# A four-layer graph network on 100,000 nodes: the row numbers of a chunk are copied one round ahead, in two of its stages

## The reference

```python
def _ngcf_conv(x, W1, W2, src, dst, n):          # layer 1, called twice
    norm = rsqrt(deg_out[src] * deg_in[dst])
    msg = (x[src] @ W1 + x[src] * x[dst] @ W2) * norm[:, None]
    return x @ W1 + segment_sum(msg, dst, n)
...
x = layernorm(x + conv(relu(conv(x, W1_1, W2_1)), W1_2, W2_2))
...
# layer 3, the last: attention over edges in both directions and a loop at each node
logits = leaky_relu(s_node[src] + d_node[dst] + e_all, 0.2)
z = exp(logits - segment_max(logits, dst)[dst])
out = segment_sum((z / segment_sum(z, dst)[dst])[:, None] * (x @ W)[src], dst)
x = layernorm(x + out)
```

## Time and profile before

| | |
|---|---|
| median of 3 runs | 10054.14 us (10051.63 to 10055.38) |
| the profiled execution's own time | 10059.48 us |
| its span, first to last instruction | 10057.3 us |
| PE, PEld | 3022.2 us (30%), 2811.3 us (28%) |
| DVE | 6330.4 us (63%) |
| ACT | 2917.7 us (29%) |
| POOL | 6560.1 us (65%) |
| `convolve_edges1`, gathers | from 3055.3 us to 4162 us |
| `finish_edges`, gathers | from 8306.7 us to 9466 us |

### The profile page before, as it was taken

One profiled execution on the slowest core, in us unless ns is written; L12 is line 12 of the kernel. 1 busy time (PEld: TensorE's weight loads), 2 busy tenths in 40 slices (PEclk: granted clock), 3 DMA queues, 4 the chain that ended last, 5 costly groups with the idle time before them and its releaser, 6 DMA issues. The chain is left out here.

```text
span 10057.3 us, 92986 instructions
## 1 busy us (share of the span) xinstructions
PE 3022.2 (30%) x15231; PEld 2811.3 (28%) x15231; DVE 6330.4 (63%) x18443; ACT 2917.7 (29%) x8172; POOL 6560.1 (65%) x6186
## 2 busy tenths in 40 slices
PE   3233002111114666500666634444400002333300
PEld 2132001111114555400655534444400002333300
DVE  8999887666664767500665579999644435666600
ACT  5366234333333444300433312222200002223200
POOL 2334017777776777577777757777677777666577
PEclk7566555555556878755555555555555555665555
DMA  1010271111113544411544511111111113434311
GB/s 53 14 30 24 98 234 26 25 25 25 25 22 101 158 148 155 134 43 50 182 170 169 177 43 48 47 47 47 39 44 45 44 42 105 112 108 115 91 45 40
DMA packets 455154, 791.99 MB, mean 79 GB/s; under 512 B 119922, under 2 KB 149611, under 8 KB 454559
## 3 DMA queue, kind: packets, MB, share of 16 engines
q1 hardware_dynamic: 252126, 560.13, 16.7%
q0 software_dynamic: 188448, 201.53, 9.2%
q10 hardware_dynamic: 14112, 26.10, 0.7%
HBM read 388.06 MB, written 425.04 MB: 81 GB/s over the span
## 5 line engine op out<-in xcount | busy, mean ns | idle before, releaser
L1056 POOL DMA_INDIRECT e_other<-X,e_from_rows x392 | 610.9, 1558 | 279.5 <-DVE e_fin L1343 143.2
L1720 POOL DMA_INDIRECT e_mine<-T,e_from_rows x392 | 400.7, 1022 | 569.3 <-DVE e_from_rows L1767 450.8
L743 POOL COPY sort_spare<-sort_words 128x768 f32<-128x768 f32 x272 | 369.2, 1379 | 606.9 <-DVE sort_words L802 396.9
L3395 POOL DMA_INDIRECT e4s_mine<-XA,e4s_from_rows x392 | 407.9, 1041 | 231.9 <-DVE e4s_from_rows L3449 124.3
L2209 PE MATMUL e_turned<-ident,e_own_x 128*128 128x128 f32 x196 | 54.6, 434 | 1573.6 <-ACT e_own_x L2121 1573.6
L2357 POOL DMA_INDIRECT e_mine<-X,e_from_rows x392 | 406.6, 1037 | 183.1 <-issue 112.5
L3416 POOL DMA_INDIRECT out_rows<-e4s_out,e4s_to_rows x392 | 385.2, 983 | 191.0 <-issue 191.0
L2378 POOL DMA_INDIRECT G<-e_g_slot,e_to_rows x392 | 385.2, 983 | 180.6 <-issue 119.0
L2865 POOL DMA_INDIRECT X<-e_row,e_to_rows x392 | 424.8, 1084 | 119.5 <-issue 116.1
L1070 POOL DMA_INDIRECT X<-e_row,e_to_rows x392 | 401.8, 1025 | 140.9 <-issue 118.2
L3398 POOL DMA_INDIRECT e4s_other<-X,e4s_from_rows x392 | 402.2, 1026 | 129.4 <-issue 127.6
(11 more groups left out here) (693 smaller groups left out, 15698.4 us busy)
## 6 DMA issues: line engine op xcount, KB each, us to landing
XA<-e_n_xa SPq DMA_DIRECT2D x49, 1056.0 KB
e4s_n_xa<-XA SPq DMA_DIRECT2D x49, 1056.0 KB, 6.3
X<-e_n_row SPq DMA_DIRECT2D x49, 576.0 KB
T<-pl_row SPq DMA_DIRECT2D x98, 272.0 KB
X<-e_n_row SPq DMA_DIRECT2D x49, 528.0 KB, 3.0
X<-pl_x ACTq DMA_DIRECT2D x98, 260.0 KB, 2.7
e_n_x<-X SPq DMA_DIRECT2D x49, 520.0 KB
G<-e_n_g SPq DMA_DIRECT2D x49, 512.0 KB, 2.8
```

Source lines behind the costliest of these rows:

```text
L1056: gp.indirect_dma_start(out=other[:, h, j, :], out_offset=None, in_=others[:, :], in_offset=bass.IndirectOffsetOnAxis(ap=from_rows[:, h, 1 ...
L1720: gp.indirect_dma_start(out=mine[:, h, j, :], out_offset=None, in_=g.T0[:, :], in_offset=bass.IndirectOffsetOnAxis(ap=from_rows[:, h, 0, j ...
L3395: gp.indirect_dma_start(out=mine[:, h, j, :], out_offset=None, in_=g.XA[:, :], in_offset=bass.IndirectOffsetOnAxis(ap=from_rows[:, h, 0, j ...
```

## The change

In both stages VectorE's pipeline is called with one more chunk in the round. The new first one, `ahead`, is chunk r of round r, and gets the copy of row numbers; all other parts get the chunks that they got, one round later (`c0` is now chunk r-1, `c1` is r-2, and so on). The copy keeps its place among the parts of the round, and its wait. The other engines' pipelines, the tiles and the semaphores are the same. VectorE's written-out first rounds become one more.

```diff
-                def body(*c):
+                def body(ahead, *c):
                     c0, c1, c2, c3, c4 = c
                     if c3:
                         node_spread(c3)
-                    if c0:
-                        n, h, k = c0.n, c0.slot, c0.k
+                    if ahead:
+                        n, h, k = ahead.n, ahead.slot, ahead.k
                         v.wait_ge(gathered[h], k * 32 * J)
                         v.tensor_copy(from_rows[:, h, :, :], g.index[s][:, 0:2, bass.ds(n * J, J)]).then_inc(from_ready[h], 1)
...
-                stages(v, NCH, RING, SKEW, body)
+                stages(v, NCH, RING, SKEW + 1, body)
...
-                def body(*c):
+                def body(ahead, *c):
                     if c[5]:
                         norm(c[5], J)
...
-                    if c[0]:
-                        n, h, k = c[0].n, c[0].slot, c[0].k
+                    if ahead:
+                        n, h, k = ahead.n, ahead.slot, ahead.k
                         v.wait_ge(gathered[h], k * 32 * J)
                         v.tensor_copy(from_rows[:, h, :, :], g.index[s][:, 0:2, bass.ds(n * J, J)]).then_inc(from_ready[h], 1)
...
-                stages(v, NCH, RING, SKEW, body)
+                stages(v, NCH, RING, SKEW + 1, body)
```

## The result

The changed kernel takes 9892.84 us (median of 4 runs, 9891.55 to 9893.38), the one before 10052.88 us beside it (4 runs, 10042.53 to 10055.38). The ratio is 0.9843, 95% interval 0.9825 to 0.986: faster by 160 us. The forecast was 9916 us, 138 us faster, in a range of 9880 to 9968; the sign and the range hold, and the gain is 22 us larger than the sum said.

The account below looks back on a forecast made before the run. POOL's gathers, waiting for VectorE's copy in both stages, were taken as the bound; 153 - 12 - 3 = 138 us off the profiled 10059.5 gives 9921.5, and 5.3 us less for the median gives 9916 us, range 9880 to 9968.

Parts of the forecast that it names:

- the sum: Both stages: 153 us of waits less 12 for longer gathers and 3 for lag, 138 us faster.
- The bound: Both stages: POOL's gather stream, including its waits for VectorE's copy of row numbers, is in the critical stretch.
- The waits removed, 52 + 101 us: POOL's waits for the copy go, except each stage's first: 52 us in convolve_edges1, 101 us in finish_edges.
- issue price: On POOL, a fixed 0.3 us after each gather; comes back for each removed wait.
- The releases next in line, with 29 and 13.4 us to spare: Slot releases are there before POOL needs them: 29 us by ScalarE's copy in convolve_edges1, 13.4 us by q1 in finish_edges.
- The longer gathers, 12 us: VectorE operations now beside gathers lengthen them: 9 us in finish_edges, 3 us in convolve_edges1.
- the price of 0.27 us per microsecond: Gather lengthening of 68 us a stage, spread over some 250 us of wide two-operand VectorE operations.
- VectorE's lag, 3 us: At the end of finish_edges, VectorE lags behind POOL after loop-head stalls; taken as 3 us.
- VectorE as the pace of the last stage: Rival, chance 0.20: VectorE's round grows once it waits less; one microsecond more in 40 rounds gives 9956 us.

Follow-up runs that it names:

- pay4: Changed kernel with the last stage's pay_out product made three more times in every round, into an unread tile; 9936.05 us.
- end_of_round_b: Changed kernel with the copy for the same chunk ahead moved to the end of VectorE's round, in both stages; 9954.75 us.
- pay2: Changed kernel with the last stage's pay_out product made once more in every round, into an unread tile; 9913.31 us.
- conv_only_b: Kernel before with the change in the first convolution alone, run again beside 10048.9 us; 9995.36 us, ratio 0.9946.
- y2: Changed kernel with the last stage's y_rows sum (one operand from PSUM) made once more in every round, into an unread tile; 9900.65 us.
- conv_only: Kernel before with the change in the first convolution alone, on the chip where the kernel before took 11692.98 us; 11705.97 us, ratio 1.0001.

## Why the prediction was right, point by point

**The bound.** Right: POOL's stream of gathers with the copy's waits in it, in both stages; on the chip of the comparison the change took out the waits and nothing else took their place.

**The waits removed, 52 + 101 us.** The waits for the copy fell by 70.6 - 12.0 = 58.6 us and by 124.3 + 1.8 - 16.3 - 3.1 = 106.7 us. Of this 6.6 and 11.4 us were to come back as issue price. Only 1.9 us did in the first stage (236.8 to 238.7 us), and in the last stage issue fell by 3.6 us (234.9 to 231.3). The rest went against another gain that the sum did not have. The prediction took the "issue" time as 0.3 us after each gather and nothing else. But some gathers had 1.5 us ahead of them, and these gaps are gone. The waits of the kernel before, then of the one after:

```profile
POOL e_got L2360 <- issue: 124.3, 392, 1.5
...
POOL e4s_other L3398 <- issue: 127.6, 386, 1.5
```

```profile
POOL e_got L2360 <- issue: 119.5, 392, 0.3
...
POOL e4s_other L3398 <- issue: 116.4, 382, 0.3
```

The kernel before has 4 such gaps in the first convolution and 8 in the last stage (and one of 0.54 us), which makes 4.8 and 9.9 us over the usual 0.3. They are not at the head of POOL's loop, which comes every 64 gathers: they are 80 or 160 gathers apart, each ahead of the second gather of a chunk whose first one had waited:

```profile
8455.03 0.94 POOL L3395 DMA_INDIRECT e4s_mine<-XA,e4s_from_rows  x1 [2.15 <-DVE e4s_from_rows L3449]
8457.49 0.94 POOL L3398 DMA_INDIRECT e4s_other<-X,e4s_from_rows  x1 [1.51 <-issue]
```

They are back where POOL waits again: the longest is 1.5 us in the last stage of pay4 and in both stages of end_of_round_b. What makes them was not tried by itself.

**The releases next in line, with 29 and 13.4 us to spare.** Right on the chip of the comparison: neither appears after the change. The one behind q1 shows 1.3 us in pay2, and comes to 30.9 us only when VectorE is slowed by some 2 us a round (pay4).

**The longer gathers, 12 us.** This term was mis-sized, by 9.5 us. In the last stage the gathers are busy 820.2 us after 810.1: +10.1, where 9 were worked out from L3509 now lying beside them, and L3509 is indeed where it came from (3.4 to 14.8 us). In the first convolution they are busy 803.7 after 811.3: -7.6 us where +3 was expected. Together +2.5 and not +12. Five traces have the same first convolution (after, conv_only_b, y2, pay2, pay4), and their gathers are busy 803.7 to 809.0 us, so a part of this is chance of phase. Most of the fall lies beside L2502, 13.8 us before and 7.7 after. That the last stage's 9 came out is in part luck as well: the price of 0.27 us per microsecond is a mean over places in the round, and pay2 and pay4 break it.

The Trainium skill (SBUF — State Buffer, "Who interferes with whom") infers that a `tensor_tensor` does not stall descriptor generation. That does not hold here: indirect gathers take 0.94 us alone and 1.83 us beside one with both operands in SBUF (the fence of y2 above). That it takes two SBUF operands to contend, which the same section says, agrees with y2's added sum, beside which no gather is over 3 ns longer.

**VectorE's lag, 3 us.** From the last gather to the end of the span it was 591.3 us (10057.3 - 9466.0) and is 593.5 (9890.7 - 9297.2): 2.2 us.

**The sum again.** 58.6 - 1.9 + 7.6 = 64.3 us and 106.7 + 3.6 - 10.1 = 100.2 us, less 2.2, and 3.9 us between the stages and ahead of them: 166.2. The profiled executions are 10059.48 - 9892.84 = 166.6 us apart. The forecast for them was 138; of the 28 us missed 14.2 (4.7 and 9.5) are the issue that did not come back, the largest part and one that the prediction put at nothing; 9.5 are the lengthening (2.5 in place of 12), 3.9 the parts between the stages, and 0.8 the lag. Both large parts erred to the same side. The medians are 160 us apart, 6.6 less, since the profiled execution before lies above all timed runs beside it.

**The rivals.** VectorE as the pace of the last stage was no bad rival: with the change its waits for gathers beyond the first chunks are 28 us, and one operation of 0.6 us a round more uses up half of them (66.3 us of waits in pay2, 51.6 of them for the first three chunks). On the other chip VectorE is the later one in the first convolution already.

## What to carry to other kernels

Where two engines wait for each other by turns, take the ring apart: copy to use, use to next copy, divided by the rounds that it spans, beside each engine's own pace. A small producer step (here 0.17 us) that stands behind a wait in a busy engine's queue is worth moving ahead by as many microseconds as the slowest round is late, not by the mean. More lead than that brought nothing on the chips near 10050 us. Where the engine that makes the copy was itself the later one (conv_only), a lead of one round brought nothing. Before moving it, look up which other releases the consumer needs, and how much earlier they are there.

## What the runs showed of the hardware that was not expected

- Some gathers have 1.5 us of "issue" ahead of them in place of 0.3. These gaps are there only in stages where POOL otherwise waits (12 in the two stages before, none after), and always ahead of the second gather of a chunk whose first one had waited; they do not fall on POOL's loop head.
- The same program took 10053 us on one chip and 11693 us on another, with gathers of the same 944 ns median, and with engines that wait for a releaser that the trace only calls "remote".
- What a wide VectorE operation with two SBUF operands costs a gather runs from nothing to about 1 us, by where it starts: node_out's 1.22 us cost 0.32 us in the mean when they start 0.2 to 0.6 us after a gather's start (after the change), and 0.93 us when they start just ahead of the next one (y2). Adding more VectorE operations can make the sum smaller (835.3 us in pay2, 816.7 in pay4).
